# The second norm of a fused two-layer block moved from VectorE to ScalarE, with products and copies reordered

## The reference

```
xn = layernorm(x)
x  = x + scan_mixer(xn) + expert_ffn(xn)        # layer 0
         scan: xi,z = xn W_in; B,C from xi; h_t = a_t h_(t-1) + B xi; (C h + D xi) * silu(z) W_out
         ffn : one of 8 experts by argmax, gelu, with a norm of its own
xn = layernorm(x)
x  = x + attention(xn) + recurrent_ffn(xn)      # layer 1
         attention: scores * decay * level factor, times V; o = Y Wout + xn
                    (o - mean o) * rsqrt(var o + 1e-5) * ln_g + ln_b      <- the "second norm"
         recurrent : three gates per step, c = tanh/sigmoid cell over the 16 blocks; tanh(x wo + c uo + bo)
```

## Time and profile before

| what | value |
|---|---|
| median of 3 runs | 990.27 us (989.64 to 991.49) |
| profiled execution | 990.02 us, its span 988.2 us |
| one steady stage | 58.45 us (L760 of `levels(i, 3)` starts at 448.99 and at 507.44) |
| busy, whole run | PE 927.3 us (94%), weight loads 683.0 (69%), VectorE 832.4 (84%), ScalarE 702.4 (71%), GpSimd 254.6 (26%) |
| granted TensorE clock | 0.989 on average |
| chain that ended last | PE 56%, VectorE 24%, ScalarE 8% |

### The profile page before, as it was taken

The page is one execution under the profiler, slowest core; times in us unless marked ns, Lnnn a source line. Parts: engine busy times, 40 slices in busy tenths (PEclk is TensorE's granted clock), DMA queues, the critical chain, the costliest instruction groups (busy, mean ns, idle before and its releaser), DMA issues.

```text
span 988.2 us, 27082 instructions
## 1 busy us (share of the span) xinstructions
PE 927.3 (94%) x9981; PEld 683.0 (69%) x9981; DVE 832.4 (84%) x2112; ACT 702.4 (71%) x1575; POOL 254.6 (26%) x321
## 2 busy tenths in 40 slices
PE   6898999999999999999999999999999999999994
PEld 3665867767676776767767686776758677676763
DVE  5888797988979798897979979798897979889776
ACT  4575785949669495875949578594966849497684
POOL 0034031220323123031321313132032312203358
PEclk9989999999999999999999999999999999999997
DMA  4000000000000000000000000000001000000527
GB/s 164 12 11 2 23 2 23 11 11 21 0 32 0 21 11 11 21 0 32 0 21 11 0 32 0 31 1 21 11 0 32 0 21 11 11 21 0 203 75 215
DMA packets 31913, 27.70 MB, mean 28 GB/s; under 512 B 1552, under 2 KB 25744, under 8 KB 31760
## 3 DMA queue, kind: packets, MB, share of 16 engines
q1 hardware_dynamic: 31888, 27.37, 8.5%
HBM read 15.57 MB, written 11.80 MB: 28 GB/s over the span
## 4 chain that ended last, share of the span: by engine, by line
PE 56%; DVE 24%; ACT 8%; issue 6%; POOL 3%; DMA 1%; DVEq 0%; ACTq 0%; SPq 0%; POOLq 0%
PE p L650 5%; PE p L652 5%; PE p L651 5%; PE p L746 3%; PE p L715 3%; PE p L524 2%; PE p L688 2%; PE p L525 2%; PE p L526 2%; DVE lv L1771 2%; DVE y L1599 2%; ACT L963 2%; DVE y L1591 2%; DVE th L1596 2%; PE p L583 2%
## 5 line engine op out<-in xcount | busy, mean ns | idle before, releaser
L1138 ACT ACTIVATE gx<-p 128x512 f32<-128x512 f32 x256 | 146.1, 599 | 1.9 <-PE p L652 0.7
L650 PE MATMUL p<-x1Th,Gl 128*128 128x512 f32 x256 | 108.2, 423 | 6.0 <-ACT gx L1138 6.0
L1180 ACT ACTIVATE yu<-p,head_part 128x128 f32<-128x128 f32 x64 | 23.5, 367 | 121.8 <-PE p L782 121.7
L652 PE MATMUL p<-x1Th,Gh 128*128 128x512 f32 x256 | 101.0, 394 | 0.0
L651 PE MATMUL p<-x1Tl,Gh 128*128 128x512 f32 x256 | 100.7, 393 | 0.0
L2022 POOL TENSOR_TENSOR vp<-vdw,e 128x256 f32<-128x256 f32 (+3 forms) x80 | 55.1, 721 | 165.5 <-DVE ms L1700 165.5
L782 PEld LDWEIGHTS p<-pair,vbd 64*32 64x32 f32 x4096 | 44.6, 105 | 42.7 <-issue 42.6
L715 PEld LDWEIGHTS p<-rs,GT 128*128 128x128 f32 x512 | 60.7, 191 | 15.6 <-ACT ms L1226 13.4
L729 PE MATMUL p<-gx,x1T 128*32 128x512 f32 x512 | 68.2, 605 | 2.1 <-DVE pair L1755 2.1
L2034 POOL TENSOR_TENSOR xnTl<-xnT 128x1 fp32r<-128x1 f32 x15 | 2.9, 193 | 258.0 <-DVE pair L1655 258.0
L1226 ACT ACTIVATE ms<-p 128x120 f32<-128x120 f32 x256 | 48.2, 278 | 23.9 <-PE p L715 21.0
(11 more groups left out here) (348 smaller groups left out, 2796.0 us busy)
## 6 DMA issues: line engine op xcount, KB each, us to landing
xin<-in_x SPq DMA_DIRECT2D x16, 256.0 KB, 2.8
hx_scratch<-vdw SPq DMA_DIRECT2D x15, 256.0 KB, 2.5
res_scratch<-normed SPq DMA_DIRECT2D x14, 256.0 KB, 2.0
gx<-in_weights SPq DMA_DIRECT2D x1, 1216.0 KB, 10.1
vp<-hx_scratch SPq DMA_DIRECT2D x4, 256.0 KB, 3.6
GT<-res_scratch SPq DMA_DIRECT2D x4, 256.0 KB, 3.6
out<-vp SPq DMA_DIRECT2D x4, 256.0 KB, 2.9
W<-in_weights SPq DMA_DIRECT2D x1, 746.0 KB, 11.2
```

What stands on the lines that cost most here:

```text
L650: pe.matmul(head_bank(h)[:, :], tile(Gl, h), x1Th[:, :], start=True, stop=False)
L652: pe.matmul(head_bank(h)[:, :], tile(Gh, h), x1Th[:, :], start=False, stop=True).then_inc(R["gx_ps"], 1)
L1138: act.activation(tile(gx, h, T), head_bank(h)[:, :], ACT.Copy).then_inc(R["gx_copied"], 1)
```

## The change

ScalarE applies the second norm: `skip = ob * r + shift`, with r the reciprocal deviation and `shift = -mean * r` for each row, which VectorE writes in one small instruction right behind `level_weights`. The four ScalarE instructions stand behind the gate's two tanh and ahead of `first_part(i, 1)`. In the place that the norm leaves on VectorE, `level_products(i, 2)` moves ahead of `other_parts(i, 2)`.

Besides: VectorE's first scan output moves from behind the four `pair_lams` to right behind the scans. ScalarE's `delta` is cut in two, with one head copy between the pieces. On TensorE all three `recurrence` products come first, then the cell's part of gate 0, `turn_x1`, and the cell's parts of gates 1 and 2; ScalarE's second recurrence tanh moves behind the copies of the turned x, and `high_part` now waits for `parts_read`. In the last block `cell_out` moves in front of head 10 and `level_weights` behind `node_rows`; there the norm stays on VectorE. Two semaphores of the setup become one.

```diff
+        shift2 = sb("shift2", TILES)
...
-                pe.matmul(P0[n][:, :], tile(gates_xh, n), x1Th[:, :], start=False, stop=False)
+                mm = pe.matmul(P0[n][:, :], tile(gates_xh, n), x1Th[:, :], start=False, stop=False)
+                if n == 2:
+                    mm.then_inc(R["parts_read"], 1)
...
                         recurrence(i, j, 0)
                         recurrence(i, j, 1)
+                        recurrence(i, j, 2)
                         recur_cell(i, 0)
+                if j is not None:
+                    turn_x1(j)
+                if i is not None:
+                    if j is not None:
                         recur_cell(i, 1)
-                if j is not None:
-                    turn_x1(j)
-                if i is not None:
-                    if j is not None:
-                        recurrence(i, j, 2)
                         recur_cell(i, 2)
...
-                heads(i, 4, H)
+                heads(i, 4, 10)
                 cell_out()
+                heads(i, 10, H)
...
+            def norm2(i):
+                act.wait_ge(R["shift_ready"], i + 1)
+                for n in range(TILES):
+                    last = act.activation(tile(skip, n), tile(ob, n), ACT.Identity, bias=shift2[:, n:n + 1],
+                                          scale=sm2[:, 4 + n:5 + n])
+                last.then_inc(R["n_ready"], 1)
...
                 if later(i):
-                    act.wait_ge(R["g_ps"], i)
+                    act.wait_ge(R["parts_read"], i)
...
                 if j is not None:
-                    delta(j)
-                if i is not None:
-                    heads(i, 8, 10)
+                    delta_size(j)
+                if i is not None:
+                    heads(i, 8, 9)
+                if j is not None:
+                    delta_log(j)
+                if i is not None:
+                    heads(i, 9, 10)
...
                     gate_tanh(j, 1)
                 if i is not None:
+                    if later(i):
+                        norm2(i - 1)
                     first_part(i, 1)
...
                         recurrence(i, 0)
-                        recurrence(i, 1)
                     turned1(j)
                     chunk_order(j)
                     high_part(j)
                     if i is not None:
+                        recurrence(i, 1)
                         recurrence(i, 2)
...
+            def norm2_shift(i):
+                dve.wait_ge(R["r2_ready"], i + 1)
+                dve.scalar_tensor_tensor(shift2[:, :], view(mv2[:, :], "p (k s) -> p k s", s=2)[:, :, 0], -1.0, sm2[:, 4:8],
+                                         ALU.mult, ALU.mult).then_inc(R["shift_ready"], 1)
...
                     scans(j)
+                    scan_out(j, 0)
...
                 if j is not None:
-                    scan_outs(j)
+                    scan_out(j, 1)
                     top1(j)
                 if i is not None:
                     level_weights(i)
+                    if later(i):
+                        norm2_shift(i - 1)
                     pair_weights(i, 1)
...
                 if i is not None:
-                    if later(i):
-                        norm2(i - 1)
+                    level_products(i, 2)
                     other_parts(i, 2)
-                    level_sum(i, 2)
+                    level_total(i, 2)
                     pair_weights(i, 3)
...
                 fold_own(i)
-                level_weights(i)
                 node_lams(i)
                 cell_out()
                 node_rows(i)
+                level_weights(i)
```

More of the change, by code:

```diff
@@ L256, in build @@
         END_BANKS = (P0[0], P0[1]) * 3 + (P0[0], P1[0])
-        names = """ident_loaded front_loaded products_loaded consts_loaded heads_loaded loaded folded setup_ps setup_ev bias_ready G_ps G_ready Gh_ready Gl_ready gates_xh_ready gates_xl_ready
+        names = """ident_loaded front_loaded products_loaded consts_loaded heads_loaded loaded folded setup_ps setup_ev bias_ready G_ps G_ready setup_high_ready Gl_ready gates_xl_ready
             x_loaded st0_ready mv0_ready ln0_steps r0_ready vr_steps q0_ready rr_ready xn_ready xh_ready
@@ L263, in build @@
             sz0_ready sz1_ready y0_ready y1_ready u0_ps u1_ps g0_ready g1_ready out0_ps x1_ready
-            st1_ready mv1_ready ln1_ready r1_ready xn1_ready x1T_ps x1T_ready x1P_ready x1Th_ready x1Tl_ready vdw_ps vdw_ready hx_stored
+            st1_ready mv1_ready ln1_ready r1_ready xn1_ready x1T_ps x1T_ready x1P_ready x1Th_ready x1Tl_ready parts_read vdw_ps vdw_ready hx_stored
             lam_steps lam_ready dt_in dt_act dt_steps g_ready gsum_steps cgT_ps cgt_ready cgc_ps
@@ L268, in build @@
             s_ps lam_ps dlam_ready w_ready vbd_zero vbd_ready y1_ps yu_ready yc_ready lev_ps lev_ready
-            yt_ready ytT_ps ytT_ready wo_ps ob_ready st2_ready mv2_ready ln2_ready r2_ready n_ready
+            yt_ready ytT_ps ytT_ready wo_ps ob_ready st2_ready mv2_ready ln2_ready r2_ready shift_ready n_ready
             res_init skip_ready ng_ready xsplit_ready hsplit_ready csplit_ready wsplit_steps res_ready normed_free f_ps i_ps g_ps tf_ready ti_ready tg_ready ig_ready c_ready
@@ L897, in stages @@
                     if j is not None:
-                        recurrence(i, j, 2)
+                        recur_cell(i, 1)
                         recur_cell(i, 2)
@@ L981, in heads_high_part @@
                 for half in range(2):
-                    act.activation(tile(Gh, half, 1024), tile(pair, half, 1024), ACT.Copy).then_inc(R["Gh_ready"], 1)
+                    act.activation(tile(Gh, half, 1024), tile(pair, half, 1024), ACT.Copy).then_inc(R["setup_high_ready"], 1)
             def first():
@@ L994, in first @@
                 turned_h(0)
-                delta(0)
+                delta_size(0)
+                delta_log(0)
                 act.wait_ge(R["setup_ps"], 3)
@@ L1014, in first @@
                 act.wait_ge(R["heads_loaded"], 16)
-                act.activation(gates_xh[:, :], w("gates_x"), ACT.Copy).then_inc(R["gates_xh_ready"], 1)
+                act.activation(gates_xh[:, :], w("gates_x"), ACT.Copy).then_inc(R["setup_high_ready"], 1)
                 heads_high_part()
@@ L1051, in turned_h, with delta_size @@
                 act.activation(xhT[:, :], P0[1][:, :], ACT.Copy).then_inc(R["xhT_ready"], 1)
-            def delta(j):
+            def delta_size(j):
                 act.wait_ge(R["delta_ps"], j + 1)
@@ L1058, in delta, with delta_log @@
                 act.activation(sp0[:, :], P0[0][:, :], ACT.Abs).then_inc(R["sp0_steps"], 1)
+            def delta_log(j):
                 act.wait_ge(R["sp0_steps"], 3 * j + 1)
@@ L1455, in gates_low_part @@
                 step(dve.tensor_scalar(neg_a1[:, :], neg_a1[:, :], -1.0, None, ALU.mult))
-                dve.wait_ge(R["gates_xh_ready"], 1)
+                dve.wait_ge(R["setup_high_ready"], 1)
                 dve.tensor_tensor(gates_xl[:, :], w("gates_x"), gates_xh[:, :], ALU.subtract).then_inc(R["gates_xl_ready"], 1)
             def heads_low_part(half):
-                dve.wait_ge(R["Gh_ready"], half + 1)
+                dve.wait_ge(R["setup_high_ready"], half + 2)
                 dve.tensor_tensor(tile(Gl, half, 1024), tile(pair, half, 1024), tile(Gh, half, 1024), ALU.subtract)\
@@ L1478, in first @@
                 scans(0)
-                scan_outs(0)
+                scan_out(0, 0)
+                scan_out(0, 1)
                 gate0(0, 0)
@@ L1585, in scans, with scan_out @@
                         .then_inc(R[f"h{q}_ready"], 1)
[L1587 to L1592, removed]
+            def scan_out(j, q):
+                dve.wait_ge(R[f"c{q}_ps"], j + 1)
+                dve.wait_ge(R[f"h{q}_ready"], j + 1)
+                dve.tensor_tensor(tile(y, q, T), P0[(2, 0)[q]][:, :], tile(y, q, T), ALU.mult)\
+                    .then_inc(R[f"ch{q}_ready"], 1)
             def gate0(j, q):
```

1 line of the change is left out of this document (removed).

## The result

The changed kernel takes 974.65 us (973.09 to 976.27), the kernel before on the same chip 990.86 (989.64 to 991.49): a ratio of 0.9838 [0.9818, 0.9858], 16.2 us faster. The forecast was 980.7 with a range of 967 to 989.5. Direction and range held; the gain came out some 6 us larger. The profiled execution took 974.35 us with a span of 972.5, so 15.7 less than the span before, where 9.6 was forecast; the granted clock is 0.989 in both.

What follows compares the result with a forecast made beforehand. VectorE sets the pace: TensorE waits 1.47 us for it ahead of `levels(i, 3)`. Net 0.67 - 0.07 = 0.60 a stage times 14 is 8.4, plus 0.8 (stage 0) and 0.4 (last block): 9.6 off 990.27, 980.7 us, range 967 to 989.5.

Steps and rivals of the forecast that it cites:

- ScalarE's four: The norm's four ScalarE instructions behind the gate's tanh: 1.5 us, bounds 1.1 and 1.84, ending near 500.6, at no cost.
- The price of the port: GpSimd's earlier chain holds off VectorE's two-SBUF-operand gate product of half 1: loss 1.05 us a stage, bounds 0 and 2.2.
- The shift: One small added VectorE instruction on 128x4, taken to cost 0.17 us a stage.
- The tail: Reordered stage end: later recurrence tanh delays ScalarE's queue to `values`; cost 0.07 us a stage, bounds -0.3 and 0.3.
- The scan output's 0.60: First scan output moved into VectorE's 0.83 us idle ahead of L1741: everything behind the second comes 0.60 us earlier.
- the reordered level product's 0.26: On VectorE, L1789 follows the level product rather than preceding it, so L1771 ends 0.26 us earlier.
- the last block: level_weights leaves the front of node_lams, so GpSimd's closing chain starts earlier: gain 0.4 us, bounds 0 and 0.67.
- the front: Stage 0, without a second norm, has only the 0.60 and 0.26 moves: gain 0.8 us taken of 0.86.
- GpSimd comes first: Rival: GpSimd starts before the gate product of half 0, which loses 1.14 us; 996.6 or 988.0 us; chance 0.22.
- The port costs nothing: Rival: GpSimd does not hold VectorE off, so the 1.47 us wait goes whole: 969.5 or 965.7 us; chance 0.15.
- The table load: Rival: ScalarE's four need table loads before and after, 1.28 us each; +3.7 us or near 1009; chance 0.03.
- The moves cancel out: Rival: tail slip of 0.3 and port cost of 1.4 eat the 1.72 us gain: 990 us; chance 0.07.

Runs made afterwards that it cites:

- e1: The changed kernel with the second norm back on VectorE and no shift instruction, all other moves kept: 975.79 us, ratio 0.9855.
- e6: The changed kernel with the order of the stage's tail undone (turn of x1, second recurrence tanh, high part's wait): 974.92 us, ratio 0.9849.
- e5: The changed kernel with the first scan output's product back in its old place behind pair_lams: 992.28 us, ratio 1.0018.
- e7: The changed kernel with ScalarE's delta in one piece again: 975.21 us, ratio 0.9843.
- e8: The changed kernel with the last block's order undone (level_weights ahead of node_lams, cell_out behind all heads): 974.38 us, ratio 0.9839.
- e3: The changed kernel, with GpSimd's residual also waiting until VectorE's gate product of half 1 is done: 964.17 us, ratio 0.9731.
- e2: The kernel before, with only the second norm moved to ScalarE and its shift on VectorE, no other moves: 997.51 us, ratio 1.0072.

## Why the prediction was right, and where its sizes were off

**The mechanism.** It was forecast that GpSimd's chain would come beside the gate, that VectorE would be first at half 0 (untouched, 0.69) and that GpSimd's third instruction would meet the product of half 1. All of it is in the timeline. The forecast had ScalarE's four end 0.24 after the product of half 0 begins (500.6 and 500.36); they end 0.42 after it (493.36 and 492.94), and L2120 starts 0.49 after it. VectorE's idle time ahead of what was L1741 shrank from 0.83 to 0.26 (L1762 at 481.68; forecast about 0.2), so the scan output is covered. The Trainium skill (SBUF — State Buffer, section Who interferes with whom) states an exclusive lock on the ports that VectorE and GpSimd share, and that nothing else contends. On the lock the trace agrees: VectorE is held off for 0.89 and GpSimd for 0.31, and the second of these no row of before had shown.

**The price of the port**, the term of 1.05 a stage (the 0.06 at L1599 is contained in it): it measured 0.89, and 0.01 at L1620, so 0.90. The step took L2036 to start only at the recorded end of L1620. The rows show it underway earlier: it ended at 497.98, so its 1.28 began at 496.70, and L1620 ended at 496.85. The handover overlaps by 0.15 in this direction too; I had used it in only one. That is 0.15 x 14 = 2.1 us of the missing 6.

**The shift**, a cost of 0.17: its record took 0.16, but it delays the next instruction by 0.07 only (see e1). The step took the length of a small instruction for its cost. That is 0.10 x 14 = 1.4 us.

**The tail**, a cost of 0.07: e6 shows a gain of 0.08. The step that failed is the choice within its bounds of -0.3 and 0.3. I followed ScalarE's queue to `values`, and that came out as forecast (4.83 after the turn against 4.79). But I took this queue for what the next norm waits for. In e6, and before, that was VectorE's L1521 (L1499 there, which ended at 464.82, and the norm's first step came at 464.85), which hangs on the turned copies; and to these I had given no weight. That is 0.15 x 14 = 2.1 us.

Together they are 0.40 a stage, 5.6 us of the missing 6. With the measured terms the sum of a stage is 0.60 - 0.07 + 1.03 + 0.26 - 0.90 + 0.08 = 1.00, as measured. TensorE's view divides the same 1.00 otherwise: the wait ahead of `levels(i, 3)` fell by 0.87 in place of the forecast 0.67, and 0.13 lies outside it.

**The other terms.** The scan output's 0.60 and the reordered level product's 0.26 are right in their sum: e1, which has these and neither the norm's move nor a lock, gains 58.44 - 57.49 = 0.95 a stage, and 0.60 + 0.26 + 0.08 is 0.94. The 0.60 also stands in the sum of e5; the 0.26 was never undone alone. ScalarE's four were put at 1.5 and took 1.64: each 0.48, so the second pointer adds 0.11 to the 0.37 of L1195, not 0.09. It changed nothing, since the cover held. (The estimate from the Trainium skill, ScalarE: Activation LUTs, section What ACT_TABLE_LOAD costs, had been 1.64; the trace agrees.) Delta in two pieces was put at nothing, and e7 shows nothing (57.44 in both). The reading that only the wait at L688 would grow was incomplete: a wait at L525 of 0.3 came as well. For the last block 0.4 was taken; e8 and the kernel before both show about 0.5. For the front 0.8 was taken; the change shows 1.3, but the seven kernels whose first scan output stands where the change has it average 111.7 there, and the three with the old place 112.5, which speaks for 0.8 or 0.9, with a scatter larger than that.

**The rivals.** That GpSimd comes first was given 0.22, and rightly not less: VectorE's lead was 0.49 us, and e5, which takes 0.60 of lead away, makes the whole change worth nothing (992.3 against 990.6). There is some luck in it: the forecast lead was 0.24 only, and with ScalarE's four at their lower bound of 1.1 instead of 1.5 GpSimd would have been first. "The port costs nothing" would have been 969.5 or 965.7; e3 builds that world and finds 964.2. The table load doesn't appear. "The moves cancel out" needed a port price of 1.4 and a tail cost of 0.3; the price was smaller and the tail a gain. (Its 990 also leaves out the 1.2 us of the ends, which make it 988.8.)

**What each part is worth in a stage**, of 1.00 in all: moves 0.94 (0.60, 0.26, 0.08), norm, shift and port together 0.05 or 0.06, the delta split nothing. The parts don't add freely, though: without the first scan output's move the norm's move costs far more than it does with it. From e1 to the change it gives 0.05; in e2 it adds 58.98 - 58.44 = 0.54.

**Left open:** where the scatter of the front comes from, and what the reordered level product is worth by itself. The sums above agree with the stage lengths to 0.01 us, which is as fine as they can be read.

## What to carry to other kernels

Before moving work off VectorE, look at whom the moved result releases: here it released GpSimd into VectorE's two-operand products, and a norm that took 1.03 us away gave 0.05. Where VectorE sets the pace and GpSimd has time to spare, hold GpSimd back with a wait of its own until the critical two-operand instruction is done; it was worth 10 us here, more than half of all that the change brought. And in such a spot compare start times to a tenth of a microsecond: with VectorE 0.49 us ahead or 0.11 behind, a stage differed by 1.16 us, of which only 0.60 is the later start itself.

## What the runs showed of the hardware

- The hold-up between VectorE and GpSimd goes both ways, and shows as a longer duration of whoever came second: VectorE's L1624 0.69 to 1.58, 1.72 or 1.74, L1620 0.75 to 1.18; GpSimd's L2036 1.28 to 1.59, L2115 0.61 to 1.07, L2124 1.28 to 1.50. Busy shares count it as work: VectorE 832.4 us before and after, GpSimd 254.6 and 267.2.
- The one held off effectively begins (its recorded end less its undisturbed length) before the recorded end of the one ahead: VectorE 0.14 us (L1624 in the change and in e5; 0.2 behind GpSimd's copy in e5), GpSimd 0.15 us (L2036, L2115, and L2124 in e5).
- In e5 L1620's record begins at 506.29, 0.02 ahead of that of the copy L2115, which follows L2036 (until 506.37) at once; yet the copy took its usual 0.61 and L1620 was the one held off. In e2 it was the same, 0.03 apart. So close together, the recorded starts don't tell who goes first.
- Two VectorE instructions beside GpSimd that weren't held off, one that reads PSUM and one with a single input: L1792 kept its 0.62 under L2036 in e3, and the reduction L1801 took 0.60 under L2124 in the change.
- `Identity` with a scale and a bias per row ran among the gate's tanh and gelu with no table load, 0.48 us for 128x128 and 1.64 for four in a row.
